# Scratch writes on two queues, rotations issued before the left halves, and an earlier index add in a one-core CIN kernel

## The reference, cut to what matters

```python
e = jnp.stack([tbl_0[ids[:, 0]], ..., tbl_31[ids[:, 31]]], axis=1)      # (1024, 32, 64) embeddings
# compressed interaction network, two layers of 128:
z = einsum('bhd,bmd->bhmd', h, x0).reshape(batch, H * M, dim)
out = relu(einsum('bcd,oc->bod', z, W) + b)
# layer 0: h = x0 = e (32 x 32 pairs); its first 64 rows are layer 1's h (64 x 32 pairs)
# the other 64 rows of layer 0 and all 128 of layer 1 are summed over dim
h = concatenate([sums, dense_ctx], axis=1)
h = maximum(h @ W_top1 + b_top1, 0); h = maximum(h @ W_top2 + b_top2, 0); y = h @ W_top3
```

## Time and profile before

| | us |
|---|---|
| median of 3 runs | 2044.36 |
| lowest, highest | 2043.90, 2044.72 |
| the profiled execution | 2043.91 |
| its span, first to last instruction | 2042.1 |

### The profile page before, as it was taken

One profiled execution on the slowest core, in us unless ns is written; L12 is line 12 of the kernel. 1 busy time (PEld: TensorE's weight loads), 2 busy tenths in 40 slices (PEclk: granted clock), 3 DMA queues, 4 the chain that ended last, 5 costly groups with the idle time before them and its releaser, 6 DMA issues.

```text
span 2042.1 us, 27494 instructions
## 1 busy us (share of the span) xinstructions
PE 1996.7 (98%) x6856; PEld 1292.0 (63%) x6856; DVE 1791.6 (88%) x1227; ACT 1545.1 (76%) x1814; POOL 1729.7 (85%) x708
## 2 busy tenths in 40 slices
PE   2999999999999999999999999999999999999998
PEld 1666666666666666666666666666666666666664
DVE  3899899899999999999999999999999999999981
ACT  2787777777777777777777777777777777877873
POOL 3988888888888888988888888888888888888871
PEclk9999999999999999999999999999999999999999
DMA  7987787787787787787787787887787787787720
GB/s 191 230 208 182 182 188 182 184 187 182 182 188 182 184 186 183 183 187 182 185 186 181 183 188 182 185 186 182 182 188 182 185 185 184 182 187 183 183 55 0
DMA packets 268303, 364.11 MB, mean 178 GB/s; under 512 B 107505, under 2 KB 107889, under 8 KB 268162
## 3 DMA queue, kind: packets, MB, share of 16 engines
q1 hardware_dynamic: 258338, 352.61, 75.2%
q0 software_dynamic: 8192, 8.40, 1.8%
q10 hardware_dynamic: 1760, 2.96, 0.5%
HBM read 347.02 MB, written 16.78 MB: 178 GB/s over the span
## 4 chain that ended last, share of the span: by engine, by line
PE 97%; SPq 1%; DMA 1%; POOL 0%; ACT 0%; issue 0%; DVE 0%
PE out L624 52%; PE out L615 21%; PE out L608 21%; PE out L610 1%; SPq L260 0%; PE out L673 0%; PE hrep L673 0%; DMA fields_dram<-emb 0%; SPq L285 0%; SPq L270 0%; POOL zl L218 0%; DMA first_row_sb<-in_first_row 0%; PE out L666 0%; PE z L666 0%; PE hrep L666 0%
## 5 line engine op out<-in xcount | busy, mean ns | idle before, releaser
L218 POOL TENSOR_TENSOR zl<-prod,zh 128x2048 fp32r<-128x2048 f32 (+1 forms) x384 | 1475.0, 3856 | 144.8 <-ACT zh L373 115.8
L624 PE MATMUL out<-zh,w1h 128*128 128x512 f32 x1536 | 652.3, 425 | 3.9 <-POOL zl L218 3.9
L373 ACT ACTIVATE zh<-prod 128x2048 fp32r<-128x2048 f32 (+1 forms) x384 | 608.2, 1618 | 4.3 <-DVE prod L542 4.2
L624 PE MATMUL out<-zl,w1h 128*128 128x512 f32 x1536 | 600.3, 391 | 0.0
L624 PE MATMUL out<-zh,w1l 128*128 128x512 f32 x1536 | 598.1, 389 | 0.0
L386 ACT ACTIVATE hrep<-out,b_sb 32x512 f32<-32x512 f32 (+1 forms) x768 | 496.3, 646 | 41.2 <-PE out L610 31.3
L608 PE MATMUL out<-prod,w_sb 128*128 128x512 f32 x1024 | 463.8, 596 | 35.2 <-DVE prod L495 30.3
L615 PE MATMUL out<-prod,w_sb 128*128 128x512 f32 x1024 | 460.1, 592 | 0.9 <-ACT relu L379 0.9
L495 DVE TENSOR_TENSOR prod<-xr,rot_low 128x2048 f32<-128x2048 f32 x128 | 292.6, 2286 | 123.3 <-PE out L610 100.6
L379 ACT ACTIVATE relu<-out,b_sb 128x512 f32<-128x512 f32 x128 | 88.0, 687 | 384.2 <-PE out L624 384.2
L624 PEld LDWEIGHTS out<-zh,w1h 128*128 128x128 f32 x1536 | 288.8, 188 | 91.2 <-issue 30.4
(11 more groups left out here) (52 smaller groups left out, 792.5 us busy)
## 6 DMA issues: line engine op xcount, KB each, us to landing
rot_low<-fields_dram SPq DMA_DIRECT2D x512, 256.0 KB
rot_high<-fields_dram SPq DMA_DIRECT2D x512, 256.0 KB
xrep<-fields_dram SPq DMA_DIRECT2D x256, 128.0 KB
fields_dram<-emb SPq DMA_DIRECT2D x512, 32.0 KB
left_x<-fields_dram SPq DMA_DIRECT2D x256, 64.0 KB, 2.3
left_y<-fields_dram SPq DMA_DIRECT2D x256, 64.0 KB, 2.2
emb<-in_tables,idx POOLq DMA_INDIRECT x256
w_sb<-in_w ACTq DMA_DIRECT2D x1, 1024.0 KB
```

What stands on the lines that cost most here:

```text
L218: pool.tensor_tensor(zl[u][:, :, :], product[:, 0:SIZES[u], :], zh[u][:, :, :].bitcast(F32), ALU.subtract).then_inc(zl_made[u], 1)
L373: act.activation(zh[u][:, :, :], product, ACT.Copy).then_inc(zh_made[u], 1)
L624: mm = nc.tensor.matmul(out1[:, :], w[:, k, :], z[:, t, :], start=False, stop=stop and t == SIZES[u] - 1 and part == 2)
```

## The change

1. Block 0's scratch writes are shared out: SP issues the four with c = 0, ACT the four with c = 1. Block 1's eight writes all go from SP to ACT, where they stand ahead of `copy_x(0, 0)`.
2. On SP block 0's `rot_low` now comes ahead of its `xrep`. Block 1's scratch writes and the load of `rot_high[1]` no longer stand ahead of block 1's `xrep`; `rot_low[2]` and `rot_high[1]` stand right behind it, ahead of `left_x` and `left_y`.
3. On POOL, in odd steps, `number_rows` and its wait for the scratch move from behind the three `low_part`s to ahead of them, right behind the gathers.

```diff
                 if is_up_to(i, c, LAST - 2 * AHEAD):
                     gathers(i, c)
-                low_part(m, 0, prod[1])
-                low_part(m, 1, prod[2])
-                low_part(m, 2, prod[3])
                 if c % 2 and is_up_to(i, c, LAST - 2 * AHEAD - 2):
                     n, b = i * 2 + c // 2 + AHEAD + 1, (c // 2 + AHEAD + 1) % 2
                     pool.wait_ge(scratch_written[b], (i + (c // 2 + AHEAD + 1) // 2) * WRITTEN)
                     number_rows(n, b)
+                low_part(m, 0, prod[1])
+                low_part(m, 1, prod[2])
+                low_part(m, 2, prod[3])
...
+        def write_copy(queue, n, b, g, c):
+            row = c * FIELDS + g * GROUP
+            queue.dma_start(
+                fields_dram[row:row + GROUP, bass.ds(n * COLS, COLS)].rearrange("f (r d) -> r f d", d=DIM),
+                emb[b][:, g, :]).then_inc(scratch_written[b], 16)
...
-            write_scratch(0, 0, 1)
+            sp.wait_ge(gathered[0], 16 * GATHERS)
+            for g in range(GATHERS):
+                write_copy(sp, 0, 0, g, 0)
             sp.wait_ge(scratch_written[0], WRITTEN)
+            load_low(0, 0)
             load_xrep(0)
-            load_low(0, 0)
             load_left(0, left_x, 0, left_x_loaded)
             load_left(0, left_y, LEFT, left_y_loaded)
             load_low(1, 1)
             load_high(0, 0)
-            write_scratch(1, 1, 1)
-            load_high(1, 1)
             sp.wait_ge(scratch_written[1], WRITTEN)
             sp.wait_ge(xr_copied, 2)
             load_xrep(1)
+            load_low(2, 2)
+            load_high(1, 1)
             sp.wait_ge(left_copied, 1)
             load_left(1, left_x, 0, left_x_loaded)
             sp.wait_ge(left_made, 1)
             load_left(1, left_y, LEFT, left_y_loaded)
-            load_low(2, 2)
             load_low(3, 3)
             write_scratch(2, 0, 2)
...
             act.wait_ge(bias_loaded, 32)
+            act.wait_ge(gathered[0], 16 * GATHERS)
+            for g in range(GATHERS):
+                write_copy(act, 0, 0, g, 1)
+            act.wait_ge(gathered[1], 16 * GATHERS)
+            for g in range(GATHERS):
+                for c in range(2):
+                    write_copy(act, 1, 1, g, c)
             copy_x(0, 0)
```

More of the change, by code:

```diff
@@ L258, in write_scratch @@
                     for c in range(2):
[L259 to L262, removed]
+                        write_copy(sp, n, b, g, c)
             def load_rotations(m, high, tile, loaded):
```

## The result

The changed kernel takes 2047.43 us (median of 22 runs, 2046.10 to 2048.75), against 2044.26 for the kernel before (22 runs beside it). The ratio is 1.0015, 95% interval 1.0008 to 1.0021: 3.2 us slower, where +1.7 was forecast. That is inside the stated range (to 2048.5) and just outside the sum's own range of +0.5 to about +3. The profiled execution has a span of 2044.6 us, against 2042.1.

The account below looks back on a forecast made before the run. PE was taken to bound the steps, and DMA throughput the prologue before `split(0, 0)`. Terms of -2.6 (shared writes), +4.3 (load order) and 0 (POOL) gave +1.7 on 2044.36, so 2046.1 us, range 2043.0 to 2048.5.

Parts of the forecast that it names:

- the sum's own range: Whole kernel: the summed terms' bounds put the change in time at +0.5 to about +3 us.
- The bound: Whole kernel: time is the start of `split(0, 0)`, then 54.02 us, plus a PE-bound rest of 15.30 us per step.
- The low clock: First `split` group: PE's granted clock of 0.60 after idling stays, the group taking 10.28 us against 8.20 later.
- Part 1: Prologue, block 0's scratch writes: sharing them between SP and ACT brings all loads forward, -2.6 us.
- Part 2: Prologue, SP's load order: `rot_low[2]`, 1.05 MB, now ahead of block 1's `left_x` delays its landing, +4.3 us.
- The sum: Landing of block 1's `left_x`: -2.6 + 4.3 = +1.7 us, carried on to the start of `split(0, 0)`.
- The block 0 order: Block 0's loads: `rot_low` before `xrep` moves the same bytes in another order, 0 us.
- POOL's part: Odd steps on POOL: the earlier index add and its wait cost 0 and gain 0.
- Sharing: Block 0's scratch writes: the rival had the shared issue gain nothing, +4.3 us, 2048.7 us; chance 0.13.
- The engines ran at 244 GB/s, not 262: Prologue loads: the rival had the DMA engines move 262 GB/s, -0.4 us in all, 2044.0 us; chance 0.15.
- that rival: SP's load queue: block 1's `left_x` overtakes the rotations and lands near 39, -4.6 us, 2039.8 us; chance 0.10.

Follow-up runs that it names:

- e1: The kernel before with only POOL's index add and its wait moved ahead of the three subtractions of odd steps: 2044.39 us, ratio 1.0000.
- e8: The changed kernel with `rot_low[1]` loaded ahead of block 0's `left_x` and `left_y`: 2046.22 us.
- e4: The changed kernel with block 1's `left_x` and `left_y` loaded ahead of `rot_low[2]` and `rot_high[1]`: 2037.97 us.
- e5: The changed kernel with `rot_low[2]` moved behind block 1's `left_x` and `left_y`, `rot_high[1]` staying right behind `xrep`: 2042.38 us.
- e9: The kernel before with `rot_high[1]` moved from ahead of block 1's `xrep` to behind its `left_x` and `left_y`: 2049.37 us.
- e10: The changed kernel with ACT's copy of block 1's `left_x` moved from ahead of step 0's first rounding to the step's end: 2039.10 us.
- e6: The changed kernel with `rot_low[3]` also loaded ahead of block 1's `left_x`: 2052.39 us.
- e2: The kernel before with only the scratch writes changed (block 0's shared, block 1's on ACT), SP's load order as before: 2042.63 us.
- e7: The changed kernel with block 0's `xrep` loaded ahead of its `rot_low` again: 2047.25 us.
- e11: The kernel of e4 with ACT's copy of block 1's `left_x` moved right behind step 0's first rounding: 2038.30 us.

## Why the prediction was right, and where it missed

- **The bound** (PE's period untouched, the start of `split(0, 0)` decides) held in the main: from the end of the first group on, every trace from e1 to e8 has the 1977.8 us of before, within 0.1. In e1, e4 and e5 PE waits once more inside that group, for POOL's second `zl`, which the start alone leaves out. In e9 and e10 DVE's step 1 came late as well. The low clock, which the prediction kept as it was, did stay (10.36 us for the first group).
- **Part 1**, forecast -2.6. From SP's first write to its first load it took 18.48 - 11.95 = 6.53 us and now 15.71 - 11.15 = 4.56: -2.0. The missing 0.6 is in the writes: ACT's four took until 14.07, 2.9 us instead of 2.6, and the landing came 1.69 us later instead of 1.42:

```profile
11.21 0.65 ACTq L254 DMA_DIRECT2D fields_dram<-emb  x1
...
11.90 2.17 ACTq L254 DMA_DIRECT2D fields_dram<-emb  x3
```

```profile
15.76 0.20 POOL L197 TENSOR_TENSOR idx<-ids_sb,first_row_sb 128x4 int32<-128x4 int32 x1 [0.86 <-DMA fields_dram<-emb]
```

- **Part 2**, forecast +4.3 for one rotation. From the first load to ACT's copy it was 46.94 - 18.48 = 28.46 us and is 33.64: +5.2. The price of the bytes was right in the mean (4.3 us per rotation over e4 to e6). Half a microsecond more may be the gap from 26 to 27 us, which I had not foreseen: block 0's left halves are issued at 64 KB per 0.6 us, less than the engines move, and by 26 us the engines had caught up with the issuing. e8's landing, 0.6 us sooner, fits that. The split between the parts is no finer than this, though. With part 1 alone (e2) the same stretch takes 45.09 - 15.89 = 29.20 us, and against that part 2 costs 4.4; e2 has a smaller gap too, with a share of 0.72. What is left over beyond 4.3 is within what two traces differ by.
- **The sum**: -2.0 + 5.2 = +3.2, where -2.6 + 4.3 = +1.7 stood. The sign and the mechanism were right; both terms were too favourable, each by under 1 us, and that put the sum at about half of what was measured.
- **A reading that was too simple.** I took the prologue before the change to be bound by bytes. The chain of waits of before has this between 35 and 47 us:

```profile
35.82 4.84 DMA fields_dram<-emb
...
44.37 2.55 DMA left_x<-fields_dram
```

That is, SP's wait for block 1's writes, then issuing, then a short landing. e9 shows it binds: 1.05 MB less ahead of `left_x` gained nothing. So the prediction added 4.3 us of bytes to a landing that bytes did not set. That it still came out is luck: the two bounds nearly coincide. With the wait gone and the same bytes, e5 has 44.52 - 15.96 = 28.56 us from first load to copy and e2 29.20, against 28.46.
- **The block 0 order** (0) and **POOL's part** (0): e7 and e1 show both.
- **The rivals.** Sharing gained 1.9 us (e2), so it does work. The prediction took the trace of before to agree that it saves issuing time; in that trace no two queues wrote at once, and e2 is the first to show it. The engines ran at 244 GB/s, not 262. `left_x` overtook no rotation (e6). What an early `left_x` would have been worth is seen in e4, where the order makes it early: 6.6 us, where that rival put 4.6. The page of the Trainium skill that was weighed there (DMA: Bandwidth & Descriptors, "Queues, rings and completion order") states that completion is not first-in first-out per issuing engine. Here nothing as large as one rotation was overtaken: behind one more of them `left_x` came 4.1 us later (e6).

## What to carry to other kernels

Once this prologue's loads were issued without a stop, the DMA engines became the bound (a share of 1.04 from 17 to 50 us), and `left_x` landed in the order of the queue. In such a case put first what an engine waits for first, and count the bytes ahead of it. Before moving a load forward, look which smaller load it now stands in front of, and which engine's later work is queued behind that one's wait; here 2.1 MB ahead of 0.26 MB cost almost 10 us (e4 against the changed kernel). The same wait can also be moved on the waiting engine, behind work that doesn't need it (e10). And a part that costs nothing in one version can cost something in a faster one, as the index add seems to in e11.

## What the runs showed of the hardware that I had not expected

While ACT issued scratch writes (16.36 to 21.47 in the changed kernel), SP's loads took longer to issue: four DMAs of `xrep` took 2.55 us there, 0.6 each, and 1.74 in the kernel before, where ACT issued nothing. It was mostly the second load that took longer, whichever it was: in e2, with the two exchanged, `xrep` took 1.76 and `rot_low` 2.56:

```profile
15.89 1.76 SPq L283 DMA_DIRECT2D xrep<-fields_dram  x4
17.69 2.56 SPq L273 DMA_DIRECT2D rot_low<-fields_dram  x4
```

So two queues' issues may not be quite independent, at up to 0.2 us per issue here; in e5 the same `xrep` took 2.00 us, 0.07 more per issue than in the kernel before. It is not shown that ACT's issuing is the cause: from 42.30 on SP's eight scratch writes took 6.27 us in the changed kernel, against 5.17, and ACT issued nothing then. The longer issues of `xrep` cost nothing that the time shows.
